# Moving five steps of a conv-attention front to other attention slots, on one Trainium2 core

## What is computed

```python
qkv = einsum('oc,bcn->bon', w_qkv, x) + b_qkv          # channel attention, 8 heads of 24 channels
q, k = l2norm(q), l2norm(k)                            # over the 1024 positions
out = einsum('bhde,bhen->bhdn', softmax(q @ k.T * temperature), v)
x = x + w_proj @ out + b_proj
t = to_tokens(x)                                       # (32, 1024, 192)
z = layernorm(t)
q, k, v = z @ Wq, z @ Wk, z @ Wv                       # 6 heads of 32
t = t + softmax(mask(q @ k.T / sqrt(192))) @ v         # causal over the tokens
h = gelu(quantize(layernorm(t) @ sign(W1).T + b1))     # quantize: absmax of groups of 6 images
t = t + quantize(h @ sign(W2).T + b2)
```

## Time and profile before

| | |
|---|---|
| median of three runs | 4434.95 us |
| lowest, highest | 4434.21, 4440.96 us |
| the profiled execution's own time | 4435.83 us |
| its span | 4434.0 us |
| PE busy | 3979.8 us, 90% |
| DVE, ACT, POOL busy | 3055.0 us (69%), 2969.4 us (67%), 363.8 us (8%) |
| mean granted clock of TensorE | 0.979 |

### The profile page before, as it was taken

The page is one execution under the profiler, slowest core; times in us unless marked ns, Lnnn a source line. Parts: engine busy times, 40 slices in busy tenths (PEclk is TensorE's granted clock), DMA queues, the critical chain, the costliest instruction groups (busy, mean ns, idle before and its releaser), DMA issues.

```text
span 4434.0 us, 114786 instructions
## 1 busy us (share of the span) xinstructions
PE 3979.8 (90%) x39240; PEld 2906.6 (66%) x39240; DVE 3055.0 (69%) x5559; ACT 2969.4 (67%) x6669; POOL 363.8 (8%) x375
## 2 busy tenths in 40 slices
PE   5999999879999898999999879999898999999888
PEld 4777774667777646777774667777646777774666
DVE  5666776766666677666766766666677666766776
ACT  2777776667776655777776667776655777776666
POOL 1000002000000110000002000000110000002000
PEclk8999999999999999999999999999999999999999
DMA  3111111011211101111111011211101111111011
GB/s 74 37 37 38 43 37 29 0 51 43 57 41 37 37 0 44 37 37 44 38 37 29 0 51 44 57 40 37 37 0 44 37 37 44 37 37 29 0 44 44
DMA packets 48832, 161.01 MB, mean 36 GB/s; under 512 B 12612, under 2 KB 13126, under 8 KB 48198
## 3 DMA queue, kind: packets, MB, share of 16 engines
q1 hardware_dynamic: 48326, 154.40, 14.5%
HBM read 28.52 MB, written 25.17 MB: 12 GB/s over the span
## 4 chain that ended last, share of the span: by engine, by line
PE 67%; DVE 13%; issue 11%; ACT 5%; POOL 1%; DMA 1%; DVEq 1%; ACTq 1%; SPq 0%; POOLq 0%
PE PT L698 12%; PE OUT L718 10%; PE S L684 7%; DVE nmax L1231 5%; PE PT L824 5%; PE S L743 5%; PE S L794 3%; PE S L642 3%; PE FR L642 3%; PE FR L586 2%; DVE work L385 2%; ACT work L952 1%; PE FR L649 1%; DVE XT L1100 1%; PE S L686 1%
## 5 line engine op out<-in xcount | busy, mean ns | idle before, releaser
L1231 DVE TENSOR_REDUCE nmax<-S 128x1 f32<-128x384 f32 (+7 forms) x1536 | 1147.7, 754 | 885.2 <-PE S L686 872.3
L952 ACT ACTIVATE work<-S,nmax 128x384 f32<-128x384 f32 (+7 forms) x1536 | 1137.0, 741 | 534.6 <-DVE nmax L1231 525.0
L698 PE MATMUL PT<-ident,work 128*128 128x128 f32 x6912 | 1068.9, 278 | 90.1 <-DVE work L385 59.6
L698 PEld LDWEIGHTS PT<-ident,work 128*128 128x128 f32 x6912 | 745.3, 142 | 242.5 <-ACT work L952 53.9
L385 DVE COPY work<-PT 128x512 f32<-128x512 f32 x768 | 524.4, 683 | 34.5 <-PE PT L698 27.5
L944 ACT ACTIVATE work<-PT 128x384 f32<-128x384 f32 (+3 forms) x768 | 335.9, 437 | 143.5 <-PE PT L698 131.8
L684 PE MATMUL S<-KS,QS 128*128 128x512 f16 (+3 forms) x1152 | 321.5, 334 | 99.5 <-ACT work L952 66.7
L684 PE MATMUL S<-odd 128*128 128x512 f16 (+3 forms) x1152 | 315.9, 329 | 59.9 <-ACT work L952 58.7
L686 PE MATMUL S<-causal,identb 128*128 128x128 bf16 x1536 | 339.0, 221 | 0.0
L956 ACT ACTIVATE work<-PT 128x128 f32<-128x128 f32 (+3 forms) x768 | 332.1, 432 | 1.4 <-PE PT L698 1.2
L743 PE MATMUL S<-odd,W1b 128*128 (+1 forms) x1080 | 259.6, 393 | 49.5 <-ACT work L995 41.2
(11 more groups left out here) (209 smaller groups left out, 6008.8 us busy)
## 6 DMA issues: line engine op xcount, KB each, us to landing
X<-in_x SPq DMA_DIRECT2D x32, 768.0 KB, 5.3
odd<-hi_z SPq DMA_DIRECT2D x128, 192.0 KB, 4.2
odd<-odd SPq DMA_DIRECT2D x128, 192.0 KB, 4.3
out_y<-work SPq DMA_DIRECT2D x64, 384.0 KB, 3.7
QS<-hi_z SPq DMA_DIRECT2D x64, 192.0 KB, 4.1
QS<-odd SPq DMA_DIRECT2D x64, 192.0 KB, 4.1
KS<-hi_z SPq DMA_DIRECT2D x64, 192.0 KB, 4.3
KS<-odd SPq DMA_DIRECT2D x64, 192.0 KB, 4.5
```

Source lines behind the costliest of these rows:

```text
L698: last = tr(bank[:, P * (j - c0):P * (j - c0) + P], PS[m % 2][:, m // 2 % 2, P * j:P * j + P], ident[:, :])
L952: A(PS[n % 2][:, n // 2 % 2, 0:w], S[:, n % 2, 0:w], ACT.Exp, bias=nmax[:, n % MAXES:n % MAXES + 1], accum_out=rowsum[:, sum_col(n):sum_co ...
L1231: v.tensor_reduce(nmax[:, n % MAXES:n % MAXES + 1], S[:, n % 2, 0:P * (qtile(n) + 1)], AX.X, ALU.max, negate=True).then_inc(max_made, 1)
```

## The change

Only the two tables change. `z3` goes from slot 34 to 33, beside `z2`. `qk0` goes from 35 to 34. `v0` to `v3` go from 41-44 to 42-45, so that slots 35 and 41 hold no step. The roundings go from slot 28 to 29 and from 29 to 30. No instruction is added, removed or resized.

```diff
 SLOTS = {"xt0": 0, "xt1": 1, "xt2": 2, "xt3": 4, "g0a": 5, "g0": 6, "g1a": 7, "g1": 8, "wg0": 9, "wg1": 10,
          "na": 11, "rb": 15, "u": 18, "mt": 19, "t0": 20, "t1": 21, "t2": 22, "t3": 23, "z0": 31, "z1": 32,
-         "z2": 33, "z3": 34, "qk0": 35, "qk1": 36, "qk2": 37, "qk3": 38, "qk4": 39, "qk5": 40, "v0": 41, "v1": 42,
-         "v2": 43, "v3": 44}
+         "z2": 33, "z3": 33, "qk0": 34, "qk1": 36, "qk2": 37, "qk3": 38, "qk4": 39, "qk5": 40, "v0": 42, "v1": 43,
+         "v2": 44, "v3": 45}
 
 SMALL_SLOTS = {"norms": 12, "rdiag": 13, "logits": 16, "xexp": 17, "attn": 17.5, "ln_stats0": 22, "ln_stats1": 25,
-               "ln_norm0": 27, "ln_norm1": 28, "ln_round0": 28.5, "ln_round1": 29}
+               "ln_norm0": 27, "ln_norm1": 28, "ln_round0": 29, "ln_round1": 30}
```

## The result

The changed kernel takes 4444.2 us (median of 20 runs, 4431.32 to 4453.59) against 4436.63 us for the kernel before in its 20 runs (4432.22 to 4440.96). The ratio is 1.0017 with a 95% interval of 1.001 to 1.0023: slower by 7.6 us, a fifth of the forecast 35.5. The runs of the changed kernel spread over 22 us, those of the kernel before over 9. The profiled execution of the changed kernel took 4436.5 us, less than 17 of the 20 runs, with a span of 4434.7 us and a mean granted clock of 0.980.

A forecast was written before the change was run, and what follows sets the result against it. PE, busy 90% of the span, was taken to bound the kernel; +10.4 us from the slots and +25 us from clock falls made +35.5 us on 4434.95 us, about 4470 us, range 4437 to 4484 us.

The forecast's parts named there:

- The clock: Falls of PE's granted clock behind the new gap before `qk0`, in half of the 31 fronts: 15.5 x 1.62 = +25 us.
- the price: Time lost when PE's granted clock falls to 0.50 once, up to slot 47: 1.62 us.
- the lower row: Profile row of the tails: PE waits 1.75 us and the granted clock behind it is 1.00, in all five.
- rival B: The gap before `qk0` without falls of the clock: only +10.4 +/- 8 us, 4445 us (4437 to 4454); chance 0.33.
- The walk through the slots: One image followed engine by engine: +0.35 us ordinary, +0.26 sixth, together +10.4 us, good to 8 us over all.
- gap ahead of it: PE idle before `qk0` in slot 34, waiting for ACT's copy of `z3`: 1.89 us.
- loss up to slot 36: Scores of slot 36 start at 1193.65 instead of 1192.53 in an ordinary image: 1.12 us later.
- gain of slots 46, 47: `v3` fills PE's wait before slot 47's scores for the exponentials of slot 45: 0.77 us gained per ordinary image.
- The stall of slot 31: PE's 0.72 us wait before slot 31's transposes moves into slot 32's; PE keeps only 0.12 us.
- Rival C: Not slower: PE keeps slot 31's 0.70 us as the second rounding does not wait for POOL; -7 us, 4428; chance 0.10.
- Rival D: Clock falls in nearly every front behind the gap before `qk0`, and a full loss: +61 us, 4496 us; chance 0.07.

## Why the prediction was wrong

**The clock was the step that failed.** The prediction bounded the share of fronts that fall between none, at 1.75 us, and four fifths, at 2.83 us, and then took "half of the 31 fronts". It had the price nearly right (1.62 us; measured 1.62 to 1.68 in ordinary images at a gap of 1.86 us and 1.62 by the medians at 2.16). The share was wrong: at 1.86 us it was 1, 2 and 4 of 31 in three profiles. The text itself said that the gap is nearer to the lower row and then left that row, with the reason that the frequency need not grow in a straight line. It does not, but it bends the other way: the share is still small at 1.86 us and large from 2.16 us on. So 25 us of the forecast became 2 to 6. The prediction also left the gaps of slot 40 out of the sum, as if they fell alike in both kernels. They fell four times before and once and three times in the two profiles of the changed kernel. With them the falls cost 6.5 us before and 4.5 and 8.0 us after, so that in these profiles the clock's term, taken as a whole, is near nothing.

The rival B, without falls, gave 4445 us and had a chance of 0.33, and 4444.2 us is what came. That the two are within a microsecond is luck in part: B's +10.4 us stood on 4434.95 us, the median of three runs, where 20 runs gave 4436.63, and its 10.4 us were twice the 5 us of the slots. B said that no front falls, and a few did.

**The walk through the slots held, and its difference did not.** Term by term, on the clock of the earlier trace rows:

| step | predicted | measured |
|---|---|---|
| POOL's subtraction | 1180.75 to 1182.34 | 1180.74 to 1182.33 |
| transposes of slot 31 | 1182.27 | 1182.32 |
| second rounding ends | 1182.76 | 1182.75 |
| maximum of slot 31 | 1182.68 | 1182.67 |
| `z3` starts | 1187.13 | 1187.04 |
| `qk0` starts | 1190.40 | 1190.29 |
| gap ahead of it | 1.89 us | 1.86 us |
| loss up to slot 36 | 1.12 us | 0.95 us |
| gain of slots 46, 47 | 0.77 us | 0.85 us |
| an ordinary image | +0.35 us | +0.11 us |

The loss was 0.17 us smaller. About 0.1 of it comes ahead of `qk0`: the multiplication behind the maximum of slot 31 came 0.20 us sooner, not the 0.12 taken (the text had 0.07 to 0.18), and `z3` and the exponentials of slot 33 moved up with it. The rest is behind `qk0`, where slot 35 took 1.86 us up to the next scores and not 1.94. The gain was larger because `v3` also covered 0.22 us that slot 46's transposes had spent waiting inside a merged row, less 0.14 us that slot 47 lost. Both errors are under the 0.25 us that was granted to a walk. But the forecast was a difference of 1.12 and 0.77, and a tenth of a microsecond counts 31-fold. In the sixth images the walk had +0.26 us; it missed what is lost behind slot 47, and they took +0.45. So +10.4 us became about +5.

**The smaller claims.** In both kernels the second rounding ended 0.42 us after POOL's subtraction, as the prediction took from the row. By the exclusive lock of the port pair (the Trainium skill, SBUF — State Buffer, section "SBUF: two separate sides") it would have been the rounding's full 0.56 us; the traces agree that the rounding waits for POOL, and not with that length. The stall of slot 31 did move into the transposes of slot 32, though 0.33 us stayed, because PE itself reached slot 31 earlier. No wait appeared between slots 36 and 46. The gap of slot 47 went in the ordinary images; in the sixth ones 0.28 of the 0.97 us stayed. Rival C is out: the maximum of slot 31 came 0.08 us sooner and not 0.4. Rival D is out too, with at most 4 of 31 fronts fallen.

## What to carry to other kernels

In a software pipeline with fixed slots, look for what stands between a producer and its consumer on the waiting engine. Here moving one consumer ahead of 1.94 us of independent work (scores, a transpose, the value product) turned cover into a gap, and one slot back is 1.4 us an image. A step whose result is needed late, as `v3` here, can be given to a slot in which the engine waits anyway. And where a change is a sum of terms of both signs, make each term alone: inside this change with its loss of 8 us lay a kernel that gains 38.

## What was not expected of the hardware

How often the granted clock falls behind an idle stretch of PE in the attention rises steeply with its length, but not to a fixed share: 0 of 31 fronts at 1.23 us, 7 of 93 at 1.86 (three profiles), 15 of 31 at 2.16, 16 of 31 at 2.55. The gap of slot 40, 2.83 us long, is in all eleven profiles and fell 42 times of 55; the 1.75 us gap of the tails is in all too, 55 times, and never fell. Which fronts fall follows a pattern in some kernels (every second image at 2.55 us), so that a share is not a chance for each. At 1.86 us, where few fall, a kernel's runs spread over 22 us, against 9 before, although every engine's order is fixed; at 2.55 us four runs agreed within 0.4 us.
